# A fused attention and routed-MLP layer on one Trainium2 core: where the pooled sums, the last key projections and the early maxima are made

## What is computed

```python
xn = layernorm(x)
# differential attention, 8 heads of 2 sub-heads, 8 channels each
q, k, v = xn @ Wq.T, xn @ Wk.T, xn @ Wv.T
q, k = rope(q) * 8**-0.5, rope(k)            # 16 sub-heads
probs = softmax(q @ k.T)                     # per sub-head, over 1024 keys
diff = probs[even] - lam * probs[odd]
attn = rms_norm(diff @ v) * (1 - LAMBDA_INIT) @ Wo.T
# routed MLP: one choice of 3 of 8 zones for each batch entry
pooled = xn.mean(axis=1)                     # (2, 128)
h = tanh(pooled @ W1 + b1)
w = top3_normalised(softmax(h @ W2 + b2))
zone_sum = sum_e w[:, e] * gelu(xn @ Wa[e]) @ Wb[e]
return x + attn + xn + zone_sum
```

## Time and profile before

| | us |
|---|---|
| median of 3 runs (lowest, highest) | 459.03 (458.35, 459.4) |
| the profiled execution, its own time | 458.67 |
| its span (first to last instruction) | 456.9 |
| busy in the span: PE, DVE, ACT, POOL | 436.1, 377.4, 342.8, 124.9 |

### The profile page before, as it was taken

How to read it: one execution, slowest core, us unless ns; L and a number is a source line. 1 busy time by engine, 2 the same in 40 slices (tenths; PEclk the granted TensorE clock), 3 DMA queues, 4 the chain that set the end, 5 groups by cost and what they waited for, 6 DMA issues and landing times.

```text
span 456.9 us, 7312 instructions
## 1 busy us (share of the span) xinstructions
PE 436.1 (95%) x2638; PEld 191.8 (42%) x2638; DVE 377.4 (83%) x720; ACT 342.8 (75%) x451; POOL 124.9 (27%) x143
## 2 busy tenths in 40 slices
PE   8999999999999899999999999999999999999986
PEld 6765565556565332333333333333333333332235
DVE  4875987878999689989999998998999999985235
ACT  3786634555465498889888889888989888989972
POOL 4248979877866000010010010010000001000000
PEclk9999999999999799999999999999999999999999
DMA  9636741410000500020002020000000000000003
GB/s 273 262 94 207 250 165 49 140 47 2 1 1 1 185 1 2 1 95 0 3 0 95 2 95 1 1 1 3 1 4 0 3 1 1 1 4 1 1 0 93
DMA packets 11726, 23.88 MB, mean 52 GB/s; under 512 B 1226, under 2 KB 5962, under 8 KB 11434
## 3 DMA queue, kind: packets, MB, share of 16 engines
q1 hardware_dynamic: 10952, 22.55, 14.6%
q10 hardware_dynamic: 738, 0.86, 0.7%
HBM read 14.49 MB, written 8.65 MB: 51 GB/s over the span
## 4 chain that ended last, share of the span: by engine, by line
PE 66%; ACT 11%; issue 10%; DVE 7%; POOL 4%; DMA 1%; ACTq 0%; POOLq 0%
PE ps L1178 19%; PE ps L1059 16%; PE ps L1171 11%; ACT E L667 10%; DVE part_max L765 4%; PE ps L1138 3%; PE ps L981 3%; PE ps L983 2%; PE ps L982 2%; POOL hL L465 2%; PE ps L1140 2%; PE ps L1139 2%; DMA X<-in_x 1%; PE ps L1164 1%; PE ps L1253 1%
## 5 line engine op out<-in xcount | busy, mean ns | idle before, releaser
L765 DVE TENSOR_REDUCE part_max<-ps 128x1 f32<-128x512 f32 x512 | 319.7, 680 | 41.9 <-PE ps L1059 38.0
L667 ACT ACTIVATE E<-ps 128x1024 f32<-128x1024 f32 x256 | 245.2, 1026 | 34.2 <-PE ps L1171 32.9
L1178 PE MATMUL ps<-E,Vg 128*32 128x512 f32 x1024 | 138.0, 611 | 1.2 <-ACT E L667 1.1
L1059 PE MATMUL ps<-K,Q 32*128 32x512 f32 x384 | 114.7, 477 | 1.5 <-DVE part_max L765 0.6
L1171 PE MATMUL ps<-Q,K 32*128 32x512 f32 x384 | 88.9, 486 | 6.4 <-ACT E L667 4.0
L1059 PEld LDWEIGHTS ps<-K,Q 32*128 32x128 f32 x384 | 47.9, 184 | 92.6 <-DVE part_max L765 84.8
L465 POOL TENSOR_TENSOR hL<-h,hH 128x512 fp32r<-128x512 f32 x48 | 61.4, 1287 | 12.3 <-ACT hH L636 12.1
L634 ACT ACTIVATE h<-ps 128x512 f32<-128x512 f32 x48 | 28.7, 597 | 40.4 <-PE ps L983 20.7
L1171 PEld LDWEIGHTS ps<-Q,K 32*128 32x128 f32 x384 | 36.9, 184 | 36.9 <-ACT E L667 33.3
L513 POOL TENSOR_TENSOR U<-AT,rsum 128x256 f32<-128x256 f32 x15 | 9.3, 622 | 144.1 <-DVE rsum L895 144.1
L1178 PEld LDWEIGHTS ps<-E,Vg 128*32 128x32 f32 x1024 | 20.3, 108 | 39.1 <-issue 33.1
(11 more groups left out here) (153 smaller groups left out, 390.5 us busy)
## 6 DMA issues: line engine op xcount, KB each, us to landing
K<-k_scr SPq DMA_DIRECT2D x5, 512.0 KB, 3.7
Q<-q_scr SPq DMA_DIRECT2D x5, 512.0 KB, 5.1
tab<-in_tables SPq DMA_DIRECT2D x2, 1024.0 KB, 10.2
wa_raw<-in_wa SPq DMA_DIRECT2D x6, 256.0 KB, 2.6
wb_raw<-in_wb SPq DMA_DIRECT2D x6, 256.0 KB, 2.9
X<-in_x SPq DMA_DIRECT2D x2, 512.0 KB, 7.2
k_scr<-V SPq DMA_DIRECT2D x2, 512.0 KB, 11.2
q_scr<-Q SPq DMA_DIRECT2D x2, 512.0 KB, 12.5
```

Source lines behind the costliest of these rows:

```text
L667: nc.scalar.activation(E[:, par, 2 * jj:2 * jj + 2, :].rearrange("p j t -> p (j t)"), ps[:, 2 * jj:2 * jj + 2, :].rearrange("p j t -> p (j ...
L765: nc.vector.tensor_reduce(part_max[:, tile // FC % 2, j * FC + tile % FC, sh:sh + 1], ps[:, SLOT_BANK[quad_slot(t) + k], :], AX.X, ALU.max ...
L1059: mm(ps[:, SLOT_BANK[x], :], Qs[g % KQ_BUFS][strip(j), tile % TB * P:(tile % TB + 1) * P], Ks[g % KQ_BUFS][strip(j), sh * BANK:(sh + 1) * ...
L1178: last = mm(ps[QUAD * j:QUAD * (j + 1), B_PV, :], Vg[:, par, st, j // 2, :], E[:, s % 2, k, :], start=(st == 0), stop=(st == TB - 1), skip ...
```

## The change

1. **Pooled sums.** `pool_sums` and its 32 matmul records go. The four ACT copies that make `xnH` also add up their rows (`accum_out`) into a `pooled` of four columns; the router's first product adds chunks 0, 2 and 1, 3 by two matmuls, and the factor 1/1024 goes into the `Tanh`. The front's order on PE and ACT shifts with it.
2. **Keys of batch entry 1.** `project(12)` to `project(15)` leave the units. Two stand beside the first scores, two in steps 0 and 1, each in a bank of the ring 4, 5, 7 as a slot of its own (four more slots). Their rotary goes with them on DVE; their POOL parts come after the last unit, and the high part is a POOL copy instead of an ACT one.
3. **Early maxima** go round four banks (4, 5, 2, 3, then 4, 5, 3, 0) in units 0 to 25, bank 3 being free of the projections.
4. Group 3 of K and Q is read back once 24 units have been made, group 4 after the last projection; `scratch(3)`, the keys of entry 1, is written after the maxima 1 to 3 instead of before.

```diff
-    return (4, 5, 2) if n < 22 else (4, 5, 0) if n < 26 else (4, 5, 0, 1)
+    return (4, 5, 2, 3) if n < 22 else (4, 5, 3, 0) if n < 26 else (4, 5, 0, 1)
+LATE_BEHIND = [(LEAD - 1, GJ - 1)] * 2 + [max_slots(s)[-1] for s in range(LATE - 2)]
...
-ADD_AT, LOW_AT = (3, 4, 9, 13), (6, 8, 12, 16)
-BESIDE = {6: 12, 8: 13, 10: 14, 12: 15}
+ADD_AT, LOW_AT = (3, 4), (6, 8)
...
             max_rows(0)
+            raw_next(3)
+            sp.wait_ge(g1_done, UZ * TOP_K)
+            kq_load(KQ_OWN)
+            for hx in range(1, 4):
+                max_rows(hx)
             scratch(3)
-            raw_next(3)
...
+            sp.wait_ge(proj_done, PROJECTIONS)
+            sp.sem_inc(sp_waited, 1)
...
+            for m in range(EARLY // 2, PROJECTIONS // 2):
+                rope_add(m)
+                rope_high(m)
+                rope_low(m)
...
-                nc.scalar.activation(xnH[:, c * BANK:(c + 1) * BANK], ps[:, c, :], ACT.Copy).then_inc(xh_done, 1)
+                nc.scalar.activation(xnH[:, c * BANK:(c + 1) * BANK], ps[:, c, :], ACT.Copy,
+                                     accum_out=pooled[:, c:c + 1]).then_inc(xh_done, 1)
...
+            rotary(EARLY // 2)
             for s in range(ALL_STEPS):
                 for t, k in max_slots(s):
                     reduce_slot(t, k)
+                if s < LATE - 2:
+                    rotary((EARLY + 2 + s) // 2, (s % 2,))
...
-            pool_sums(0)
+            keep_warm(2)
             pe.wait_ge(w_split, 1)
...
-            pe.wait_ge(pool_done, 1)
+            pe.wait_ge(xh_done, CHUNKS)
             pe.wait_ge(s_in, 16 * 6)
-            mm(ps[0:ROUTER, 7, 8:8 + BATCH], w1_in[:], pooled[:], start=True, stop=True).then_inc(hid_ps, 1)
-            project(5)
+            mm(ps[0:ROUTER, 7, 8:8 + BATCH], w1_in[:], pooled[:, 0:CHUNKS:CB], start=True, stop=False)
+            mm(ps[0:ROUTER, 7, 8:8 + BATCH], w1_in[:], pooled[:, 1:CHUNKS:CB], start=False, stop=True).then_inc(hid_ps, 1)
+            project(6)
...
-                if n in BESIDE:
-                    project(BESIDE[n])
...
             score(0, 1)
+            pe.wait_ge(gelu_done, UNITS)
+            project(EARLY)
             pe.wait_ge(z_out, CHUNKS)
             score(0, 2)
             score(0, 3)
+            project(EARLY + 1)
...
+                if s < LATE - 2:
+                    project(EARLY + 2 + s)
```

More of the change, by code:

```diff
@@ L104, in lead_ring @@
     n = (GJ * (t - 1) + k) // LEAD_BANKS
-    return (4, 5, 2) if n < 22 else (4, 5, 0) if n < 26 else (4, 5, 0, 1)
-def ring_tables():
-    banks, before, last = [], [], {}
-    for t in range(QUADS):
-        extra = (t % 8 == 2 and t > 2) + (t == QUADS - 1)
-        for k in range(GJ + extra):
-            bank = min(lead_ring(t, min(k, GJ - 1)), key=lambda b: last.get(b, -1))
-            before.append(last.get(bank))
-            last[bank] = len(banks)
-            banks.append(bank)
-        if t == 0:
-            last.clear()
-    return banks, before
-SLOT_BANK, SLOT_BEFORE = ring_tables()
-assert len(SLOT_BANK) == SLOTS
-def last_lead_slot(banks, steps=UNITS):
-    t, k = lead_slots(steps - 1)[-1]
-    return max(x for x in range(quad_slot(t) + k + 1) if SLOT_BANK[x] in banks)
+    return (4, 5, 2, 3) if n < 22 else (4, 5, 3, 0) if n < 26 else (4, 5, 0, 1)
 def max_slots(s):
@@ L137, in max_slots, with ring_tables, last_lead_slot @@
     return [divmod(x, 4) for x in range(up_to(s), up_to(s + 1))]
+LATE_BEHIND = [(LEAD - 1, GJ - 1)] * 2 + [max_slots(s)[-1] for s in range(LATE - 2)]
+def ring_tables():
+    users = []
+    for t in range(QUADS):
+        for k in range(GJ):
+            users.append(((t, k), lead_ring(t, k)))
+            if k == GJ - 1 and t % 8 == 2 and t > 2:
+                users.append((("half", t // 8 - 1), lead_ring(t, k)))
+            users += [(("project", EARLY + i), RING) for i in range(LATE) if LATE_BEHIND[i] == (t, k)]
+    users.append((("half", 2 * GROUPS - 1), RING))
+    slots, banks, before, last = {}, [], [], {}
+    for user, ring in users:
+        slots[user] = len(banks)
+        bank = min(ring, key=lambda b: last.get(b, -1))
+        before.append(last.get(bank))
+        last[bank] = len(banks)
+        banks.append(bank)
+        if user == (0, GJ - 1):
+            last.clear()
+    return slots, banks, before
+SLOT_OF, SLOT_BANK, SLOT_BEFORE = ring_tables()
+assert len(SLOT_BANK) == SLOTS
+def last_lead_slot(banks, steps=UNITS):
+    t, k = lead_slots(steps - 1)[-1]
+    return max(x for x in range(SLOT_OF[t, k] + 1) if SLOT_BANK[x] in banks)
 HEADS_AT = (MAX_STEPS + 4, MAX_STEPS + 5, ALL_STEPS - 3)
@@ L971, in turn @@
                 last.then_inc(xt_done, 1)
-            def pool_sums(b):
-                for n in range(b * TB, (b + 1) * TB):
-                    last = mm(ps[:, 7, 96 + b:97 + b], XN[:, n, :], cst[:, C_ONE:C_ONE + 1], start=n == b * TB,
-                              stop=n == (b + 1) * TB - 1)
-                last.then_inc(pool_ps, 1)
             def three(o, lh, ll, rh, rl, start, stop):
@@ L1065, in _ @@
             turn(1)
[L1066 removed]
+            keep_warm(2)
             pe.wait_ge(w_split, 1)
[L1068 to L1070 removed]
+            for k in range(4):
+                project(k)
             turn(2)
[L1072 removed]
+            project(4)
             turn(3)
```

92 lines of the change are left out of this document (41 added, 51 removed).

## The result

| | before | after |
|---|---|---|
| median us (lowest to highest) | 459.21 (458.35 to 461.22) | 451.94 (451.56 to 454.1) |
| the profiled execution, its own time | 458.67 | 452.07 |
| its span | 456.9 | 449.6 |
| router: first reduction to last row of the chain | 23.56 to 27.65 | 22.07 to 27.68 |
| `second(0)` | 41.76 | 42.66 |

The ratio after to before is 0.9834, 95% interval 0.9804 to 0.9864: 1.7% faster. In the span the stretches give +0.9 (front), -9.6 (`second(0)` to `second(28)`: 69.71 and 60.09), nothing from there to the last unit (38.72 in both), +1.4 (attention up to step 3), -7.3 in all. From step 3 on the distance stays (the last `probs_v` starts at 440.36 and 433.07).

A forecast was written before the change was run, and what follows sets the result against it. The router's DVE chain sets the front, PE the MLP's 2.02 us rounds when banks are free, and mostly PE attention. Terms -2.1 - 9.4 + 1.0 = -10.5 us gave 448.5 us, with 8 in 10 in 445.0 to 453.5.

The forecast's parts named there:

- rival 2: Start of attention costs its upper bound, +3.5 us, with a half clock, giving 451.0 us; chance 0.14.
- rival 1: MLP: the four-bank ring gives nothing, DVE or POOL bounds the units, which stay at 2.46; 452.9 us; chance 0.17.
- front: Up to the MLP: removing the pooled-sum matmuls before the router saves 2.1 us, bounds -1.2 and -2.4.
- (a) projections out of the units: MLP up to unit 28: four units lose their projection, 1.24 us each, -5.0 us.
- (b) fourth bank: MLP up to unit 28: late slots costing 0.44 us go from nine units, -4.0 us.
- MLP in all: second(0) to second(28): -9.4 us, bounds -5.0 and -10.4.
- start of attention: Four projections now fall here, partly offset by a fuller clock: step 3 comes 1.0 us late, bounds -0.5 to +3.5.
- so the router's chain starts near 21.5 instead of 23.56: -2.1 us: Front: without the second pooled sum the router's DVE chain starts earlier, and 2.1 us are saved.
- rival 3: Change turns out slower: PE pauses in the front, and a half clock lasts into the MLP; over 459.9 us, chance 0.03.
- The nine units: MLP up to unit 28: units counted as lengthened 0.44 us by a late slot, for -4.0 us.
- The count from the other side: MLP: 28 rounds at 2.02, start sums and transposes make 59.3 us, or -10.4; 1 us of new POOL waits gives -9.4.
- The first two projections fill that idle time: Start of attention: two projections run while PE waits for DVE's backlog and then the exponentials; each takes 0.69 us on PE.

The follow-up runs named there:

- e13: Kernel before with only the new pooled sums and the front order that goes with them; 459.16 us, ratio 0.9991.
- e4: Kernel after with the early maxima back in three banks until unit 25, projections still at attention; 459.63 us, ratio 0.9999.
- e3: Kernel after with five filler matmuls before the matmul that waits for the router; 454.26 us, ratio 0.9871.
- e9: e8 plus the POOL wait of e1 and three filler matmuls before the router's answer; 450.27 us, ratio 0.9805.
- e12: e10 plus five filler matmuls in step 0 of attention; 449.03 us, ratio 0.9757.
- e1: Kernel after with POOL holding back the second low part of the rotary until the router's picks are out; 451.25 us, ratio 0.9825.
- e8: Kernel after with the first two late projections ahead of the first attention scores; 450.88 us, ratio 0.9826.
- e5: Kernel after with the third and fourth late projections behind probs_v of steps 0 and 1 instead of before; 452.48 us, ratio 0.9863.
- e2: Kernel after with POOL holding back both first low parts of the rotary until the router's picks are out; 458.3 us, one run.
- e6: Kernel after with the pooled sums and front order of the kernel before; 454.19 us, ratio 0.9886.
- e10: e9 plus the other two late projections behind probs_v of steps 0 and 1, as in e5; 450.78 us, ratio 0.9786.

## Why the prediction was right, and where not

The direction was right, and the median of 451.94 lies in the range of 445.0 to 453.5. But it is 3.4 us over the forecast of 448.5 and outside 445.5 to 450.5, which had a chance of 0.62. It lies between rival 2 (451.0) and rival 1 (452.9), and neither of their mechanisms stood in the traced execution: what moved the time was the front. Against the profiled execution (forecast 448.2, measured 452.07) the 3.9 us are: front 3.0, MLP -0.2, attention 0.4, and 0.7 outside the span (2.5 us where before had 1.8).

| term | forecast | measured | from |
|---|---|---|---|
| front | -2.1 (-1.2 to -2.4) | +0.9; -1.1 with a full clock | after; e13 |
| (a) projections out of the units | -5.0 | -3.5 | e4 |
| (b) fourth bank | -4.0 | -6.1 | e4 |
| MLP in all | -9.4 | -9.6 | after |
| start of attention | +1.0 (-0.5 to +3.5) | +1.4 | after |

**Front: the step that failed.** The chain's start near 21.5 was about right (21.4 to 22.1 over the kernels with the new front, 22.07 in the traced after). The step "so the router's chain starts near 21.5 instead of 23.56: -2.1 us" took the chain's length for a constant. It is 4.09 us only behind POOL's low parts; the operations that it moved beside them were held for 1.5 us. The prediction named such a delay for the large `wb_zone` and did not look for it in the small operations, although the trace of before has POOL's low parts ending at 24.69, in the middle of the chain's first operations. Then the clock, half for about three us, took 1.3 more. That the pause brought the fall is likely: all five traces with fillers in it (e3, e9 to e12) have a full clock there. It is not certain: of the six new fronts without them four had the half clock (after, e1, e4, e8) and two did not (e5, e13). It would be the mechanism of rival 3, PE pausing before the router's answer, at a small part of its size: it reached no unit of the MLP. The two warm-up matmuls of the change stand at the first pause only. The accumulating copy costs one record of 0.19 to 0.20 us on ACT, inside the bound of 0.3, and hidden, as put.

**MLP: right sum, wrong split.** 60.3 us were forecast from `second(0)` to `second(28)`, and 60.09 measured; 18 of the 28 rounds are 2.01 to 2.03 us long, and rival 1 (the ring gives nothing) fell. The two terms were mis-sized in opposite directions, and the sum came out by the luck that the errors nearly cancel (+1.5 and -2.1). The excess of a unit with a projection over 2.02 us was put down to the projection alone, 1.24 us. In unit 6 it is 0.78 for the projection (3.26 to 2.48 in e4) and 0.46 for the missing bank (2.48 to 2.02); a unit behind one with a projection even got 0.1 us longer in e4 (1.91 to 2.03). The nine units were no right count either: of before's nine rounds of 2.46 to 2.50 three (units 1, 24 and 28) are as long in the kernel after, while the bank cost something in fifteen rounds of e4. The count from the other side, 59.3 us plus 1 of new waits, did not depend on the split, and held.

**Attention: near in size, with one step wrong.** "The first two projections fill that idle time" was wrong. They stand behind the first two scores, and the 1.05 us stay empty; e8 shows the price, 1.25 us. Step 0 is 2.0 us later than before where 1.4 was forecast, and step 3 is 1.4 later where 1.0 was. That is less over the forecast than e8's 1.25; what made up for the rest was not separated. The clock stayed full in the profiled execution, as hoped. `probs_v(0)` came 5.65 us after the first scores (forecast some 5), and step lengths behind step 3 are unchanged. Rival 2 (the clock falls all the same) did not come about in the profiled execution of after, but a half clock there did in those of e1, e2, e3, e5, e6, e9 and e10, which have step 3 at 15.0 to 19.7. After and e3 have the same code there, so it can differ from execution to execution, and a chance of 0.14 looks too low for it. In how many of after's own executions it came is open: the mean clocks of its four (0.989 to 0.996) say only that some part of each was at half.

## What to carry to other kernels

When a chain is moved forward in time, read what every other engine does in the stretch that it moves into: small VectorE operations can be held for a whole POOL operation, and their length in the old place is no price for the new one. Where work on TensorE is taken out or a wait is left, look for the half clock behind the pause, in several executions, and try filling a pause of about a microsecond with idle matmuls into a free bank: five of them at the start of attention made this kernel faster by 1.8 us (e10 to e12) and its times even. To split a gain between two parts, undo one alone; excesses read off single rounds may hold both.
